# Who splits the normalised rows into 16-bit planes: moving 38 copies from GpSimd to ScalarE in ten paired steps

## The reference, cut to what matters

```python
x = L0_attn_data                                           # 4 x 1024 tokens, 1024 features, fp32
x = _layernorm(x + _L0_attn_ref(x, weight, mask), axis=-1) # stage A: one 1024x1024 product, block mask
x = _layernorm(x + _L0_ffn_ref(x, ...), axis=-1)           # stage B: product, bias, LoRA
x = _layernorm(x + _L1_attn_ref(x, ...), axis=-1)          # projection, 4 layers of scan and MLP, read-out
x = _layernorm(x + _L1_ffn_ref(x, ...), axis=-1)           # stage D: product, routed LoRA

def _layernorm(x, axis=-1, eps=1e-05):
    m = jnp.mean(x, axis=axis, keepdims=True)
    v = jnp.var(x, axis=axis, keepdims=True)
    return (x - m) / jnp.sqrt(v + eps)
```

## Time and profile before

| | |
|---|---|
| median of three runs | 1653.36 us (1652.39 to 1657.66) |
| profiled execution, its own time | 1656.23 us |
| its span, first to last instruction | 1654.3 us |
| busy: PE, PEld, DVE | 1614.8, 1299.1, 1175.0 us |
| busy: ACT, POOL | 666.4, 618.5 us |
| mean granted TensorE clock | 0.988 of full speed |
| ten pairs of stage A | about 91 to 304 us of the span |

### The profile page before, as it was taken

One profiled execution on the slowest core, in us unless ns is written; L12 is line 12 of the kernel. 1 busy time (PEld: TensorE's weight loads), 2 busy tenths in 40 slices (PEclk: granted clock), 3 DMA queues, 4 the chain that ended last, 5 costly groups with the idle time before them and its releaser, 6 DMA issues.

```text
span 1654.3 us, 22809 instructions
## 1 busy us (share of the span) xinstructions
PE 1614.8 (98%) x7734; PEld 1299.1 (79%) x7734; DVE 1175.0 (71%) x2150; ACT 666.4 (40%) x987; POOL 618.5 (37%) x507
## 2 busy tenths in 40 slices
PE   8999999999999999999999999999899999999998
PEld 7877777788888888888866666676788788888886
DVE  6978888566666666568878777778767776676633
ACT  3544443443333333323345555545433333343311
POOL 4323333353333323213577777762213222221200
PEclk9999999999999999999999999999899999999999
DMA  7233333555444444543140000003546555555321
GB/s 281 78 114 102 121 102 102 183 144 131 118 120 120 119 114 125 152 113 77 46 158 27 1 1 1 1 13 115 203 147 214 193 196 188 181 203 182 138 79 51
DMA packets 140195, 196.58 MB, mean 119 GB/s; under 512 B 75954, under 2 KB 84146, under 8 KB 139826
## 3 DMA queue, kind: packets, MB, share of 16 engines
q1 hardware_dynamic: 115250, 125.92, 26.3%
q10 hardware_dynamic: 24832, 69.22, 11.0%
HBM read 105.97 MB, written 72.35 MB: 108 GB/s over the span
## 4 chain that ended last, share of the span: by engine, by line
PE 78%; DVE 10%; issue 5%; ACT 3%; DMA 2%; POOL 1%; ACTq 0%; SPq 0%; DVEq 0%; POOLq 0%
PE ps L885 15%; PE ps L887 14%; PE ps L886 14%; PE ps L1131 7%; PE ps L1073 3%; PE ps L1031 2%; PE ps L1079 2%; PE ps L1123 2%; PE ps L964 2%; PE ps L1121 2%; PE ps L1122 2%; PE ps L897 2%; PE ps L966 2%; PE ps L965 2%; PE ps L1099 1%
## 5 line engine op out<-in xcount | busy, mean ns | idle before, releaser
L2625 POOL TENSOR_TENSOR rstd<-var_eps,minus_half 128x1 f32<-128x1 f32 x96 | 89.8, 936 | 556.9 <-DVE minus_mean L1909 556.9
L885 PE MATMUL ps<-wall_x,x_hi 128*128 128x512 f32 x688 | 273.8, 398 | 4.9 <-ACT wall_x L1476 2.1
L887 PE MATMUL ps<-wall_x,x_lo 128*128 128x512 f32 x688 | 268.9, 391 | 0.0
L886 PE MATMUL ps<-wall_x,x_hi 128*128 128x512 f32 x688 | 268.8, 391 | 0.0
L885 PE MATMUL ps<-wall_y,x_hi 128*128 128x512 f32 x512 | 201.9, 394 | 0.0
L886 PE MATMUL ps<-wall_y,x_hi 128*128 128x512 f32 x512 | 199.4, 389 | 0.0
L887 PE MATMUL ps<-wall_y,x_lo 128*128 128x512 f32 x512 | 199.4, 389 | 0.0
L885 PEld LDWEIGHTS ps<-wall_x,x_hi 128*128 128x128 f32 x688 | 129.6, 188 | 34.5 <-ACT wall_x L1476 4.4
L887 PEld LDWEIGHTS ps<-wall_x,x_lo 128*128 128x128 f32 x688 | 129.5, 188 | 27.8
L886 PEld LDWEIGHTS ps<-wall_x,x_hi 128*128 128x128 f32 x688 | 129.7, 189 | 25.2
L1841 DVE TENSOR_TENSOR row<-ps,bias 128x512 f32<-128x512 f32 x128 | 87.8, 686 | 86.8 <-PE ps L887 85.5
(11 more groups left out here) (329 smaller groups left out, 3633.9 us busy)
## 6 DMA issues: line engine op xcount, KB each, us to landing
x_scratch<-row ACTq DMA_DIRECT2D x32, 512.0 KB, 2.7
x_in<-x_scratch SPq DMA_DIRECT2D x32, 512.0 KB, 4.0
out<-row ACTq DMA_DIRECT2D x32, 512.0 KB, 2.8
x_in<-in_x_t SPq DMA_DIRECT2D x29, 512.0 KB, 3.8
w_first<-in_w_t SPq DMA_DIRECT2D x56, 256.0 KB, 2.9
x_scratch<-planes_early ACTq DMA_DIRECT2D x27, 512.0 KB, 3.3
cx<-x_scratch SPq DMA_DIRECT2D x24, 512.0 KB, 4.3
x_scratch<-cx ACTq DMA_DIRECT2D x24, 512.0 KB, 3.6
```

The source lines that it names most:

```text
L885: pe.matmul(bank, hi[:, k], wall[:, k, 0, cols], start=(k == 0), stop=False)
L886: pe.matmul(bank, hi[:, k], wall[:, k, 1, cols], start=False, stop=False)
L887: return pe.matmul(bank, lo[:, k], wall[:, k, 0, cols], start=False, stop=(k == KC - 1))
L2625: pool.tensor_tensor(rstd[:, i:i + 1], var_eps[:, i:i + 1], minus_half[:, 0:1], ALU.pow)\
```

## The change: what it does

In the ten pairs the two copies of each step move from GpSimd to ScalarE, for steps 6 to 24: 19 steps, 38 copies. A new `part_planes` on ScalarE waits for the normalised row and for the landing of the previous store, copies both halves and sends them. It stands at two places in a pair: behind `op_hi(p + 1, A11)` for step a - 2, and behind `hold(p, 1)` for step a - 1. `normalise(a - 1)` and `op_hi(p + 1, A12)` now stand in front of `hold(p, 1)`, not behind it. Steps before 6 and from 25 on stay with GpSimd.

```diff
+            def part_planes(s):
+                halves = row[:, s % 2].bitcast(U16).rearrange("p (f h) -> p h f", h=2)
+                act.wait_ge(normed, norm_count(s))
+                act.wait_ge(stored[(s - 1) % 2], 16 * ((s - 1) // 2 + 1))
+                for part in range(2):
+                    act.activation(planes[0][:, part], halves[:, part], ACT.Identity).then_inc(parted, 1)
+                send_planes(s)
...
                 if p > 0:
-                    send_planes(a - 2)
-                hold(p, 1)
+                    part_planes(a - 2)
                 normalise(a - 1)
                 if more:
                     op_hi(p + 1, A12)
                 else:
                     split_x(S_END)
+                hold(p, 1)
+                part_planes(a - 1)
                 if more:
                     op_hi(p + 1, S2)
                     op_hi(p + 1, S3)
...
                 else:
                     take_b(0, 1)
-                send_planes(a - 1)
                 extra(p)
...
             for p in range(PAIRS):
                 a = S_BEG + 2 * p
-                if p > 0:
-                    part_planes(a - 2)
                 root(a - 1)
-                part_planes(a - 1)
                 root(a)
```

## The result

The changed kernel takes 1646.41 us in the median of four runs (1645.11 to 1647.18) against 1655.17 us of the kernel before (1652.39 to 1657.66, four runs). The ratio is 0.9947 with a 95% interval of 0.9926 to 0.9967. A second series of six runs gave 1646.42 us and again 0.9947 (0.9932 to 0.9962). So the change saves 8.8 us (5.5 to 12.2). The forecast was 12.4 us from 1653.36 to 1641, with a range from 1636 to 1649.5. The sign, the range and the mechanism hold; the size was 3.6 us too large, just outside the interval, and the starting point 2 us too low.

What follows compares the result with a forecast made beforehand. TensorE, busy 98% of the span, was taken as the bound, leaving only its gaps to win. -14.9 - 1.5 + 0.5 + 2.7 + 0.8 = -12.4 us, from 1653.36 to 1641 us; range 1636 to 1649.5.

Steps and rivals of the forecast that it cites:

- TensorE's gaps in front of A22: In the pairs, TensorE waits at A22 for VectorE's join: 14.9 us of waits plus 1.5 us of slow clock to win.
- late roots: Pairs 1, 5 and 7: hold now stands behind the row, so a late root holds up S1; 0.5 us loss booked together.
- The copies cost this chain 1.2 us: Pair 3: GpSimd's two copies slow VectorE's x_lo and first sum, 1.2 us together, ahead of A22.
- c = 1.06: Price of one copy on ScalarE, taken as 1.06 us from its copy of 1024 fp32 values; range 0.53 to 2.04.
- The chain in pair 3: Steps on ScalarE and VectorE up to join(3, 1), ending at 174.1 instead of 176.4; A22 due at 175.5.
- The store keeps ScalarE busy for 0.38 us: In a pair, issuing the store behind two copies takes 0.38 us, so ScalarE is free at 166.0 in pair 3.
- The last pair: 2.7 + 0.8: Last pair: pick_b waits longer for b_rows behind the copies of step 24, 2.7 us, and the clock may fall, 0.8 us.
- Behind the pairs the rest moves along: Behind the pairs all is TensorE's own work, relative to which the rest moves along, so the gain stays.
- The difference goes to the median: The profiled execution lay 2.9 us above the median; its gain was applied to the median: 1653.36 - 12.4 = 1641 us.
- late root at the hold: Rival: S1 waits in pairs 1, 5 and 7 about 2 us each instead of A22; 1646 to 1647 us; chance 0.11.
- dear copies: Rival: copies on ScalarE cost more in the chain ahead of join(p, 1); 1651 at c = 1.75, 1665 at 2.1; chance 0.09.
- upper bound of 2.04 us: Limit from above for c, one copy on ScalarE: the slowest copy of these planes on GpSimd, 2.04 us.

Runs made afterwards that it cites:

- still_copies: last_b_first with GpSimd also copying a piece of a weight tile to an unread place, 34 times, at the old times: 1645.59 us against 1639.10.
- change_again: The changed kernel once more, unaltered, in a second series: 1646.42 us, ratio 0.9947 to the kernel before.
- last_b_first: The changed kernel with take_b(0, 0) in front of hold(9, 1) and the copies of step 24 in the last pair: 1639.10 us, ratio 0.9900 to before.
- order_only: The kernel before with only the new order on ScalarE, the copies left on GpSimd: 1646.53 us, ratio 0.9943 to before.
- half_more: The changed kernel with one of the two copies made twice in steps 6 to 22, three copies a step: 1647.59 us, ratio 0.9958 to before.
- twice: The changed kernel with both copies made twice in steps 6 to 22, four copies a step: 1659.03 us, ratio 1.0024 to before.
- w_later: The changed kernel with the loads of the first two weight parts issued one step later: 1639.41 us, ratio 0.9909 to before.
- copies_b_first: The changed kernel with hold(p, 1) back in its old place and take_b(0, 0) ahead of the copies of step 24: 1638.62 us, ratio 0.9898 to before.

## Why the forecast was right in kind and too large in size

- *"TensorE's gaps in front of A22 are the only time to win, 14.9 us of waiting and 1.5 us of clock": right.* From 100.68 us to A22 of pair 8, 14.9 us were won; what is left of gaps in the pairs (from start to start 0.28 and 0.53 in front of two A22 and 0.24 in front of an S1) is 1.1 us against the 0.5 booked for late roots. Some 0.3 us of both windows of eight pairs are small matmuls in the first pair and no gap, which the prediction's 15.3 counted as lost. The half-clock stretch of the earlier trace rows is gone too.
- *"The copies cost this chain 1.2 us": right*, and still_copies is the proof. But the reason given for the plain pair was one of two: the order alone closes its gap as well. The copies are indispensable only in the long pairs, where the prediction spoke of roots.
- *"c = 1.06": right.* The 38 copies took 1039 to 1060 ns, median 1047:

```profile
L1425 ACT ACTIVATE planes_early<-row x38: 1039/1047/1060, 104.5 to 280.8; 128x1024 uint16<-128x1024 uint16 x38
```

  So ScalarE takes no longer for single 2-byte values with two bytes between them than for 1024 fp32 values side by side (1058 ns). The Trainium skill's rule ("Vector Engine (DVE) Microarchitecture Reference", section 5.2), measured there on VectorE, by which the prediction's estimate for a copy came to 1.75 us, does not hold for this instruction. The skill's page "ScalarE: Activation LUTs", section "What ACT_TABLE_LOAD costs", gives an ACTIVATE without pointer operands as 186 ns and 0.833 ns an element; the estimate of 1039 ns by it is the shortest copy of the row.
- *"The chain in pair 3": right to 0.3 us at its end, in part by luck.* S3 starts at 161.13, on before's scale 167.34, 6.21 later. There `hold(3, 1)` ends at 168.2, as before and not 1.0 us later: the shift could start at 165.6 instead of 166.55, the root being early. `join(3, 1)` ends at 174.35, forecast 174.1. The prediction's sum leaves out that `join(3, 1)` needs `hold(3, 2)`; that sets the floor, 1.15 us ahead of A22. The chain that the prediction summed ran about 1 us ahead of it: `x_lo` of A12 at 167.7 instead of 168.7, the `x_lo` of S2 and S3 done at 172.6 instead of 173.5, on before's scale. The floor hid this, and A22 was on time either way.
- *"The store keeps ScalarE busy for 0.38 us": too little.* Behind most pairs of copies the queue stands for 0.51 us (158.89 to 159.41), since the store waits for the copies to be written and the row waits behind it.
- *"The last pair: 2.7 + 0.8": right in kind, and in sum in part by luck.* `pick_b` came 3.5 us late instead of 1.1, 2.4 more, and the slow matmuls behind it took 7 x 0.2 = 1.4 us, where half of such a loss, 0.8, was booked. From A22 of pair 8 to behind them 3.7 us were given back, 3.5 forecast. In change_again it was 5.7. last_b_first shows that the whole of it was avoidable.
- *"Behind the pairs the rest moves along": false by 1.2 us* (11.4 at 334 us, 10.2 at the end; in change_again 9.7 and 6.5). The pieces at 1.2 GHz fall in other places in each execution; by the mean granted clock of the profiles, 0.987 to 0.995, they cost 8 to 21 us in all.
- *"The difference goes to the median": this step failed.* The profile of before was 2.9 us above the median of three; but that median was low, since the four series with 41 runs of the kernel before gave medians of 1654.7 to 1655.8. Of the 5.4 us between 1641 and 1646.4, 1.8 are this, 1.0 is the sum in the pairs and the last pair (12.4 against 11.4 at 334 us), 1.2 was given back behind, and 1.4 is the difference between one profile (10.2 us) and the medians (8.8).

Of the rivals, *late root at the hold* is real with GpSimd copying (order_only, still_copies), and dear copies are real from about c = 1.5 us on (half_more, twice). Neither is in the change. The c at which the prediction has the whole change turn to a loss is, by its own sum, 1.8 and not 1.9 us. Its upper bound of 2.04 us, GpSimd's slowest copy, is one that stood beside a long two-input instruction of VectorE, so it held a wait as well.

## What to carry to other kernels

When a chain on one engine has an instruction at twice the time of its like, look for what another engine does in that moment before moving anything in the chain: taking GpSimd's copies away won 13.9 us in the pairs and reordering 6.9, and both together no more than the larger. A copy moved to an idle engine is cheap until it stands ahead of something with a deadline; here one small `b_rows` behind it gave back a quarter of the gain, and the kernels that put it first are 16 to 18 us faster than before instead of 9, of which 5 us can be read off the last pair. Take the starting point from as many runs as the forecast's precision needs.

## What the runs showed of the hardware that was not expected

- GpSimd's 16-bit copies slow VectorE's two-input fp32 instructions of 512 values from 0.69 to 1.09, 1.38, 1.41 and 1.52 us, whatever data the copies touch, and one of 128 values from 0.28 to 1.12, but not `stats`, which has one input. Two copies take 2.48 us together instead of 2.02 (before, from 95.78, where VectorE has only `stats` and small work): the first keeps its 1.04 us, and the second, begun inside a VectorE instruction, takes 1.39 to 1.51. The Trainium skill, "GPSIMD Engine Reference", section 1, has GpSimd share its SBUF interfaces with VectorE, with contention where a VectorE instruction has two SBUF inputs; the rows agree, and give it its price and its form, the taking of turns above. ScalarE's copies of the same data do not slow VectorE: its sum in pair 3 of the change takes 0.69 us beside one (162.86 to 163.55).
- A store of 512 KB landed in 3.1 us in the median, in 6.0 to 6.8 beside a tile of x and two weight parts, and in 4.1 beside the tile alone.
- Behind the gap of 3.71 us TensorE's granted clock was at the level of 1.2 GHz for seven matmuls; behind gaps of 1.75 and 1.24 us (w_later, copies_b_first) in the same place it stayed at 2.4.
